# Second-layer weight remainders on VectorE, and one set of statistics for two layer norms, in an attention and mixture-of-experts kernel

## The chip, the cores and the metric

The kernel runs on one core of one Trainium2 chip. A core has TensorE for matmuls, VectorE (DVE), ScalarE (ACT) and GpSimd (POOL) for elementwise work, and SyncE (SP), which here only issues DMAs. Each engine works through its own queue in order, and engines wait for each other through semaphores. The metric is device time in microseconds (us), less is better.

## The reference, cut to what matters

The input has 4 images of 1024 tokens and 256 channels. An image goes through a group norm with attention and a projection, then, as tokens, through a second attention, and then:

```python
t = t + attention(_ln_t(t))
t = t + ffn(_ln_t(t))

def ffn(x):                       # 8 experts, the two best for each token
    x_norm = layernorm(x) * ln_g + ln_b
    combine = weights of the top 2 of softmax(x_norm @ gate_w)
    for e in range(8):
        h = gelu(x_norm @ w1[e] + b1[e])          # 256 -> 1024
        out = out + combine[:, e] * (h @ w2[e] + b2[e])   # 1024 -> 256
    return x + out
```

So two layer norms follow the attention: the first makes x out of t, the second makes x_norm out of x. Both divide by sqrt(variance + 1e-5).

## The kernel before, in words

Every large matmul is made exact enough by splitting both operands into a high half (a rounded fp32r copy) and a low half (value minus high half), and by three passes on TensorE (`three`, line 1567). The high half is usually made by ACT, the low half by DVE.

**Images.** `image` on each engine does one image, b = 0 to 3. The first attention goes over eight row blocks i: TensorE turns the probabilities (L1647), computes the scores of block i+2, and mixes the values of block i-1. On DVE block i is `lo1(i)` (L1277), `max1(i+2)` (L1272), `out1(i-1)` (L1286 to L1295), `norm1(i-2)` (L1300). TensorE's turning of block i+1 waits for `lo1(i)`. On ACT, `hi1(i)` (L812) stands before it.

**The tail of an image**, everything from the attention's sum to x_norm, is spread over the start of the next image; image 3's tail stands alone between attention and routing. It works in halves h of four token tiles. DVE adds the attention result (`tail_add`, L1227) and takes statistics (`tail_stats`, L1238 to L1243: which=0 of t, which=1 of x). POOL makes the scale by a power of -1/2 (L589) and the bias (L614, L615). ACT applies them (`tail_norm`, L776). The sum t + x for the accumulator rows is on POOL (`stream`, L621), and the multiplication by ln_g and the addition of ln_b are on POOL inside the images (`affine`, L626, L628) and on DVE in the last tail (L1462, L1465). SP writes both results to DRAM (`rows_of`: L480 for r_out, and behind it in the same queue L483 for xf). Routing starts when all five engines have signalled their end; SP's comes after both DMAs have landed.

**Routing** builds, from the gate's logits, a table of up to 40 steps, each with one expert and 256 token slots (`route`).

**Expert steps.** Step s uses buffer n = s mod 2. TensorE computes eight chunks f of the first layer, three chunks ahead, and eight of the second. ACT applies the gelu (L971); DVE makes the two halves of its result, the high half by a conversion (`tensor_copy`, L1535) and the low half by a subtraction (L1537). Between chunks, the halves for step s+1 are prepared: if its expert differs from the one in that buffer (`fresh`), both weights are loaded again, 1 MB each, and split in eight pieces of 128x512. ACT makes the high halves of all eight (L931), DVE the low halves of the four first-layer pieces (L1487, at chunks 0, 1, 3, 4) and POOL the low halves of the four second-layer pieces (`split_w2`, L729). POOL's queue also gathers rows for step s+2 (L694) and scatters those of step s-1 (L707), both by indirect DMAs; `split_w2` stands behind them. DVE also adds the second-layer bias (L1508, after chunk 1) and splits the gathered rows (L1499, after chunk 2). Two steps form a turn of a loop; each step reads `fresh` from a table and branches, and each turn reads `live` as well. The pieces of step 0 are made during routing (`first_pieces`, before L1135).

## Time and profile before

| | us |
|---|---|
| median of 3 runs | 1328.66 |
| lowest and highest run | 1323.03, 1333.6 |
| span of the profiled execution | 1323.4 |

No separate total of the profiled execution is given; its span equals the fastest run to within 0.4 us, so what lies around the span is taken as nothing.

| engine | busy us | share of the span |
|---|---|---|
| TensorE matmuls | 1184.0 | 89% |
| VectorE | 874.8 | 66% |
| ScalarE | 545.9 | 41% |
| GpSimd | 414.8 | 31% |

Up to the end of the images TensorE is busy for nine tenths or more of nearly every slice. They take the span up to about 694 us, the last tail runs to 729, routing to 782, the expert steps from there to about 1292, and the output transposes the rest. The chain that ended last is 79% TensorE and 13% VectorE; 71% is line 1567, 7% is the conversion in line 1535. A shared line such as 1567 serves many products, so the tiles beside it say which one is meant. An idle time in brackets counts for the time of the kernel only on the engine that everything else waits for.

### The profile page before, as it was taken

Reading aid. Unit: us, or ns where it says so; the run is one execution under the profiler, and the core shown is the slowest. Engines: PE = TensorE matmul, PEld = TensorE weight load, DVE = VectorE, ACT = ScalarE, POOL = GpSimd, SP = SyncE. Lnnn points to the kernel's source line nnn. Section 1 sums busy time; section 2 is a strip of 40 time slices with the busy share of each in tenths; the row PEclk is TensorE's granted clock in tenths of the full one; section 3 lists DMA queues with packets and bytes.
Section 4 is the critical chain, followed back from the end, with each engine's and each line's share of the span. In section 5 each row is a group of like instructions: output and inputs, shape, how many; then the busy total and the mean of one; then the engine's idle time right before and its main releaser. Section 6 shows DMA issues by size and latency. Waiting matters only on the chain.

```text
span 1323.4 us, 25477 instructions
## 1 busy us (share of the span) xinstructions
PE 1184.0 (89%) x8118; PEld 1099.4 (83%) x8119; DVE 874.8 (66%) x1819; ACT 545.9 (41%) x995; POOL 414.8 (31%) x416
## 2 busy tenths in 40 slices
PE   6999999999999999999993468889879897799992
PEld 5897998989889889898883368789779897799992
DVE  4675477854668537684357968866885868966651
ACT  2432445434344334543333245535544545444431
POOL 0010003400024000240003365665664566644540
PEclk9999999999999999999995688899889899999997
DMA  4000001100001000000001314525433536323337
GB/s 155 1 33 0 1 1 33 64 1 0 2 33 64 0 1 1 33 33 0 1 1 64 135 68 129 154 44 148 146 82 59 168 94 179 96 53 59 56 48 258
DMA packets 66205, 82.69 MB, mean 62 GB/s; under 512 B 11104, under 2 KB 56544, under 8 KB 66144
## 3 DMA queue, kind: packets, MB, share of 16 engines
q1 hardware_dynamic: 52128, 63.48, 14.7%
q0 software_dynamic: 14016, 18.37, 7.7%
q8 instruction: 42, 0.69, 0.2%
q14 instruction: 19, 0.16, 0.0%
HBM read 60.85 MB, written 22.02 MB: 63 GB/s over the span
## 4 chain that ended last, share of the span: by engine, by line
PE 79%; DVE 13%; ACT 2%; issue 2%; DMA 2%; SPq 1%; POOL 1%; ACTq 0%; POOLq 0%; DVEq 0%
PE ps L1567 71%; DVE hs L1535 7%; PE ps L1647 2%; PE ps L1857 1%; PE ps L1609 1%; PE ps L1580 1%; ACT h L971 1%; DVE hs L1537 1%; DVE one_hot L1122 1%; DMA rows<-acc_rows 1%; ACT w2s L931 1%; DVE pick_hi L1130 1%; PE ps L1600 1%; PE ps L1656 1%; PE ps L1669 1%
## 5 line engine op out<-in xcount | busy, mean ns | idle before, releaser
L1567 PE MATMUL ps<-w2s,hs 128*128 128x256 f32 x1728 | 265.6, 291 | 46.9 <-DVE hs L1537 46.5
L1567 PEld LDWEIGHTS ps<-w2s,hs 128*128 128x128 f32 x1728 | 235.9, 198 | 52.3 <-DVE hs L1537 50.0
L1567 PE MATMUL ps<-xt,w1s 128*128 128x256 f32 x1746 | 269.0, 292 | 3.2 <-issue 1.7
L1567 PEld LDWEIGHTS ps<-xt,w1s 128*128 128x128 f32 x1746 | 237.5, 198 | 5.0 <-issue 2.9
L1535 DVE CAST hs<-h 128x256 fp32r<-128x256 f32 x288 | 178.5, 620 | 87.7 <-ACT h L971 45.8
L971 ACT ACTIVATE h<-ps,b1t 128x256 f32<-128x256 f32 x288 | 136.8, 475 | 121.1 <-PE ps L1567 100.9
L707 POOL DMA_INDIRECT acc_rows<-y_w,now_s x72 | 117.6, 1633 | 170.1 <-issue 163.3
L1537 DVE TENSOR_TENSOR hs<-h,hs 128x256 fp32r<-128x256 f32 x288 | 124.2, 431 | 9.9
L589 POOL TENSOR_TENSOR tl_r<-tl_eps,minus_half 128x4 f32<-128x4 f32 x16 | 16.2, 1013 | 350.8 <-DVE tl_eps L1243 350.8
L1567 PE MATMUL ps<-xs,wh 128*128 128x512 f32 x384 | 123.1, 401 | 1.5 <-issue 1.5
L694 POOL DMA_INDIRECT xg<-xf_rows,now_g x76 | 86.8, 1143 | 48.1 <-POOL now_g L690 35.5
L1567 PE MATMUL ps<-vs,pr 128*128 128x256 f32 x768 | 98.1, 283 | 0.0
L1567 PEld LDWEIGHTS ps<-vk,pr 128*128 128x128 f32 x768 | 94.0, 188 | 3.2 <-DVE pr L1384 0.8
L1567 PE MATMUL ps<-xs,qs 128*128 128x512 f32 x384 | 95.5, 397 | 0.0
L1567 PE MATMUL ps<-vk,pr 128*128 128x256 f32 x768 | 94.8, 279 | 0.6 <-DVE pr L1384 0.6
L1567 PE MATMUL ps<-qs,ks 128*128 128x512 f32 x384 | 92.3, 391 | 0.0
L1567 PEld LDWEIGHTS ps<-vs,pr 128*128 128x128 f32 x768 | 92.2, 188 | 0.0
L1379 DVE TENSOR_REDUCE neg_max<-ps 128x1 f32<-128x1024 f32 x32 | 39.2, 1224 | 79.8 <-PE ps L1567 79.8
L729 POOL TENSOR_TENSOR w2s<-w2r,w2s 128x512 fp32r<-128x512 f32 x64 | 88.3, 1774 | 1.1 <-ACT w2s L931 1.1
L1567 PEld LDWEIGHTS ps<-xs,wh 128*128 128x128 f32 x384 | 69.7, 189 | 16.0 <-issue 1.7
L1567 PEld LDWEIGHTS ps<-qs,ks 128*128 128x128 f32 x384 | 70.1, 188 | 13.5
L1567 PEld LDWEIGHTS ps<-xs,qs 128*128 128x128 f32 x384 | 69.7, 188 | 13.6
(213 smaller groups left out, 1908.5 us busy)
## 6 DMA issues: line engine op xcount, KB each, us to landing
w1r<-in_w SPq DMA_DIRECT2D x16, 1024.0 KB, 5.0
w2r<-in_w SPq DMA_DIRECT2D x16, 1024.0 KB, 8.9
b2t<-in_b SPq DMA_DIRECT2D x36, 128.0 KB
xn<-in_x SPq DMA_DIRECT2D x4, 1024.0 KB, 4.9
acc_rows<-r_out SPq DMA_DIRECT2D x4, 1024.0 KB, 4.5
xf_rows<-xf SPq DMA_DIRECT2D x4, 1024.0 KB, 5.0
rows<-acc_rows SPq DMA_DIRECT2D x8, 512.0 KB, 7.4
out_tokens<-cols_out SPq DMA_DIRECT2D x8, 512.0 KB, 9.2
```

Source lines behind the costliest of these rows:

```text
L589: return g.tensor_tensor(dst, src, minus_half[:, 0:src.shape[1]], ALU.pow)
L694: g.indirect_dma_start(out=xg[:, n, h, :], out_offset=None, in_=xf_d, in_offset=bass.IndirectOffsetOnAxis(ap=now_g[:, n, h:h + 1], axis=0) ...
L707: g.indirect_dma_start(out=acc_d, out_offset=bass.IndirectOffsetOnAxis(ap=now_s[:, n, h:h + 1], axis=0), in_=y_w[:, n, h, :], in_offset=No ...
L729: g.tensor_tensor(w2s[n][1][:, :, :].rearrange("p f c -> p (f c)")[:, c], w2r[:, n, c], w2s[n][0][:, :, :].rearrange("p f c -> p (f c)")[: ...
L931: a.copy(dst[:, c], src[:, n, c]).then_inc(ws_act, 1)
L971: a.activation(h32[:, gi % 4, :], bank(gi % 4, STEP), ACT.Gelu, bias=b1t[:, n, f:f + 1]).then_inc(h_act, 1)
L1122: v.tensor_tensor(one_hot[:, j, :], iota[:, 0:COLS].unsqueeze(1).to_broadcast((P, PICK, COLS)), hi_f[:, k, t].unsqueeze(2).to_broadcast((P ...
L1379: v.tensor_reduce(neg_max[:, i:i + 1], bank(2 * (i % 2), count=2), AXX, ALU.max, negate=True).then_inc(s2_max, 1)
L1535: v.tensor_copy(hs[0][:, f, :], h32[:, gi % 4, :]).then_inc(h_hi, 1)
L1537: v.tensor_tensor(hs[1][:, f, :], h32[:, gi % 4, :], hs[0][:, f, :].bitcast(F32), ALU.subtract).then_inc(h_lo, 1)
L1567: ins = t.matmul(out, left[l], right[r], start=first and n == 0, stop=last and n == 2, **more)
L1647: ins = t.transpose(bank(4, count=2)[:, j * P:(j + 1) * P], prob[:, i % 2, j * P:(j + 1) * P], ident[:, :])
```

## The change

Two edits are made at once.

**Edit 1, expert steps.** POOL's `lo_pieces` and `split_w2` are gone. DVE subtracts all eight pieces of a fresh step, in chunks 0, 1, 3, 4, 5, 6 and 7 (two in chunk 7), and the eight of step 0 during routing. `ws_dve` now counts eight pieces.

**Edit 2, the tail.** The sum t goes to a tile of its own, `t1`. One set of statistics (mean m, variance v of t1) serves both norms: POOL raises two numbers per token, v + eps and v(1 + eps) + eps^2, to the power -1/2 in one instruction of twice the size. ACT writes the accumulator rows directly, as t1 times (1 + r) minus m r (`tail_rows`); DVE writes xf in two passes over each tile with ln_g and ln_b in them (`tail_xf`), eight instructions per half. POOL's `stream` and `affine` are gone, and ACT's pass for xf. In the last tail `tail_rows` stands behind ACT's `gate_columns`.

```diff
-        ACT_TAIL = {1: (0, 1), 3: (1, 0), 4: (1, 1)}
-        DVE_TAIL = {2: (1, 0), 3: (1, 1)}
+        DVE_TAIL = {2: 0, 3: 1}
...
+            def tail_scales(b, h):
+                c = slice(4 * h, 4 * h + 4)
+                pool.wait_ge(tl_in, at(b, 2, h + 1))
+                g.tensor_tensor(tl_r[:, :, c], tl_eps[:, :, c],
+                                minus_half[:, :].rearrange("p (k t) -> p k t", k=2), ALU.pow).then_inc(tl_own, 1)
+                pool.wait_ge(tl_own, at(b, 2, h + 1))
+                g.tensor_tensor(tl_nb[:, c], tl_nm[:, c], tl_r[:, 0, c], ALU.mult).then_inc(tl_out, 1)
+                g.tensor_tensor(tl_s[:, c], tl_r[:, 0, c], ones[:, 0:4], ALU.add).then_inc(tl_out, 1)
...
-                    lo_pieces(s + 1, 1 - n, (i if n == 0 else i + 1))
...
+            def tail_rows(b, h):
+                act.wait_ge(tl_out, at(b, 4, 2 * h + 2))
+                if not (isinstance(b, int) and b == 0):
+                    act.wait_ge(tok_out, at(b, 16, 0))
                 for j in range(4 * h, 4 * h + 4):
-                    ins = a.activation(dst[:, j, :], src[:, j, :], ACT.Identity,
-                                       bias=tl_nb[:, which, j:j + 1], scale=tl_r[:, which, j:j + 1])
-                ins.then_inc(ready, 1)
+                    ins = a.activation(r_out[:, j, :], t1[:, j, :], ACT.Identity,
+                                       bias=tl_nb[:, j:j + 1], scale=tl_s[:, j:j + 1])
+                ins.then_inc(r_ready, 1)
...
-            for which in range(2):
-                for h in range(2):
-                    tail_norm(B - 1, which, h)
             for h in range(2):
                 gate_columns(B - 1, h)
+            for h in range(2):
+                tail_rows(B - 1, h)
...
+                v.tensor_scalar(tl_eps[:, 1, cs], tl_mv[:, cs, 1], 1.0 + LN_EPS, LN_EPS * LN_EPS,
+                                ALU.mult, ALU.add)
+                v.tensor_scalar(tl_nm[:, cs], tl_mv[:, cs, 0], -1.0, None, ALU.mult)
+                v.tensor_scalar(tl_eps[:, 0, cs], tl_mv[:, cs, 1], LN_EPS, None, ALU.add).then_inc(tl_in, 1)
+
+            def tail_xf(b, h):
+                dve.wait_ge(tl_own, at(b, 2, h + 1))
...
+                for j in range(4 * h, 4 * h + 4):
+                    step(v.scalar_tensor_tensor(xf[:, j, :], t1[:, j, :], tl_mv[:, j, 0:1], g_row[:, :],
+                                                ALU.subtract, ALU.mult))
+                settle()
+                for j in range(4 * h, 4 * h + 4):
+                    ins = v.scalar_tensor_tensor(xf[:, j, :], xf[:, j, :], tl_r[:, 1, j:j + 1], b_row[:, :],
+                                                 ALU.mult, ALU.add)
+                ins.then_inc(xf_ready, 1)
...
                 def out1(i):
                     w(av_mm, NT, i + 1)
-                    if i == 0 and not first:
-                        w(r_ready, 2, 0)
...
-            W_AT = (0, 1, 3, 4)
+            W_AT = {0: (0,), 1: (1,), 3: (2,), 4: (3,), 5: (4,), 6: (5,), 7: (6, 7)}
...
             def first_pieces():
-                for f in range(4):
+                for f in range(8):
                     w_piece(0, 0, 0, f)
...
-                    if split and f in W_AT:
-                        w_piece(s + 1, 1 - n, (i if n == 0 else i + 1), W_AT.index(f))
+                    if split:
+                        for piece in W_AT.get(f, ()):
+                            w_piece(s + 1, 1 - n, (i if n == 0 else i + 1), piece)
```

What the edits do to the order of instructions, at three places. First, GpSimd in the expert loop behind the scatter, with a fresh step to come. Before (the last two rows come twice more):

```order
L707 DMA acc_rows<-y_w,now_s 4096x256 x2
L716 ISA
L716 TENSOR_LOAD fresh
L716 ISA x2
L716 COMPARE_AND_BRANCH
L723 ISA
L725 ISA
L727 REGISTER_ALU
L729 TENSOR_TENSOR w2s<-w2r,w2s 128x512
L727 REGISTER_ALU
L729 TENSOR_TENSOR w2s<-w2r,w2s 128x512
L727 REGISTER_ALU
```

and now, where the next gather follows the scatter directly:

```order
L661 DMA acc_rows<-y_w,now_s 4096x256 x2
L644 ISA
L644 COPY now_g<-gather_at 128x2
L645 REGISTER_ALU
L648 DMA xg<-xf_rows,now_g 128x256 x2
```

The table read, the branch and the four subtractions behind the scatter are gone.

Second, VectorE in chunks 6 and 7 of such a step (REGISTER_ALU rows prepare the number that the next instruction waits for). Before:

```order
L1535 CAST hs<-h 128x256
L1537 TENSOR_TENSOR hs<-h,hs 128x256
L1532 REGISTER_ALU
L1535 CAST hs<-h 128x256
L1537 TENSOR_TENSOR hs<-h,hs 128x256
```

and now:

```order
L1473 CAST hs<-h 128x256
L1475 TENSOR_TENSOR hs<-h,hs 128x256
L1423 REGISTER_ALU
L1427 TENSOR_TENSOR w2s<-w2r,w2s 128x512
L1470 REGISTER_ALU
L1473 CAST hs<-h 128x256
L1475 TENSOR_TENSOR hs<-h,hs 128x256
L1423 REGISTER_ALU
L1427 TENSOR_TENSOR w2s<-w2r,w2s 128x512
L1423 REGISTER_ALU
L1427 TENSOR_TENSOR w2s<-w2r,w2s 128x512
```

One second-layer piece now follows chunk 6 and two follow chunk 7; one more follows chunk 5.

Third, VectorE in row block i = 2 of an image that carries a tail, from `norm1(0)` to `lo1(3)`. Before:

```order
L1300 TENSOR_SCALAR tn<-tok,ln_mv,ln_r 128x256
L1238 BN_STATS tl_bn<-x 128x6 x4
L1156 REGISTER_ALU
L1161 MEMSET spare 128x1
L1241 BN_AGGR tl_mv<-tl_bn 128x2 x4
L1156 REGISTER_ALU
L1243 TENSOR_SCALAR tl_eps<-tl_mv 128x4
L1277 TENSOR_TENSOR pr<-ps,pr 128x1024
```

and now (`t` is the tile t1):

```order
L1243 TENSOR_SCALAR tn<-tok,ln_mv,ln_r 128x256
L1181 REGISTER_ALU
L1183 SCALAR_TENSOR_TENSOR xf<-t,tl_mv,g_row 128x256 x4
L1086 REGISTER_ALU
L1187 SCALAR_TENSOR_TENSOR xf<-xf,tl_r,b_row 128x256 x4
L1222 TENSOR_TENSOR pr<-ps,pr 128x1024
```

Where statistics of x stood ahead of `lo1(3)`, the eight instructions of `tail_xf(0)` stand now.

## Rows read from the trace of the kernel before

**Rows 1.** Windows with fresh weights, one and the sum of four: us, busy us per engine, PEclk.

```profile
914.90:985.20 70.30, 57.21 (x420) 55.52 (x419) 60.41 (x89) 36.28 (x78) 44.87 (x41) 0.89 0.49 142
...
sum 246.00, PE 199.69 PEld 193.58 DVE 211.75 ACT 126.11 POOL 156.59; mean PE 49.92 PEld 48.40 DVE 52.94 ACT 31.53 POOL 39.15
```

**Rows 2.** The same view: a pair of steps with reused weights, and step 0.

```profile
1218.00:1241.50 23.50, 23.50 (x202) 23.50 (x201) 14.34 (x36) 9.91 (x22) 12.02 (x12) 1.00 0.33 56
786.50:799.80 13.30, 10.99 (x87) 10.20 (x86) 12.36 (x21) 8.33 (x19) 9.88 (x10) 1.00 0.51 179
```

**Rows 3.** The same windows, conversions of line 1535 alone.

```profile
sum 246.00, DVE 118.79; mean DVE 29.70
```

**Rows 4.** The reused pair, conversions of line 1535 alone.

```profile
1218.00:1241.50 23.50, 5.33 (x16) 1.00 0.33 56
```

**Rows 5.** Instructions of line 729 (count: shortest/median/longest ns).

```profile
L729 POOL TENSOR_TENSOR w2s<-w2r,w2s x64: 1270/1827/1873, 781.3 to 1155.5; 128x512 fp32r<-128x512 f32 x64
```

**Rows 6.** Timeline of a step with fresh weights: start, duration, engine [idle before it].

```profile
924.80 6.35 DVE L1535 CAST hs<-h 128x256 fp32r<-128x256 f32 x1
...
925.47 5.52 POOL L729 TENSOR_TENSOR w2s<-w2r,w2s 128x512 fp32r<-128x512 f32 x4
...
931.67 1.03 PE L1567 MATMUL ps<-w2s,hs 128*128 128x256 f32 x6 [3.46 <-DVE hs L1537]
...
933.57 0.35 DVE L1535 CAST hs<-h 128x256 fp32r<-128x256 f32 x1 [1.96 <-PE ps L1567]
```

**Rows 7.** Timeline of VectorE a little later, back to back.

```profile
936.17 0.68 DVE L1487 TENSOR_TENSOR w1s<-w1r,w1s 128x512 fp32r<-128x512 f32 x1
936.77 0.28 DVE L1535 CAST hs<-h 128x256 fp32r<-128x256 f32 x1
```

**Rows 8.** Timeline, first row block of an attention image that carries a tail.

```profile
374.95 2.08 ACT L776 ACTIVATE x<-tok,tl_nb,tl_r 128x256 f32<-128x256 f32 x4 [1.38 <-POOL tl_nb L615]
...
377.96 1.23 DVE L1277 TENSOR_TENSOR pr<-ps,pr 128x1024 fp32r<-128x1024 f32 x1 [0.98 <-ACT pr L812]
...
379.34 1.06 PE L1647 MATMUL ps<-ident,prob 128*128 128x128 f32 x8
```

**Rows 9.** Timeline, the row blocks i = 2 and 3 of the same image.

```profile
395.02 1.40 DVE L1238 BATCH_NORM_STATS2 tl_bn<-x 128x6 f32<-128x256 f32 x4
...
396.95 1.22 DVE L1277 TENSOR_TENSOR pr<-ps,pr 128x1024 fp32r<-128x1024 f32 x1
...
399.41 1.03 PE L1647 MATMUL ps<-ident,prob 128*128 128x128 f32 x8
...
401.66 1.40 DVE L1238 BATCH_NORM_STATS2 tl_bn<-x 128x6 f32<-128x256 f32 x4
```

**Rows 10.** Instructions that write tl_r.

```profile
L589 POOL TENSOR_TENSOR tl_r<-tl_eps,minus_half x16: 1006/1014/1018, 204.1 to 707.2; 128x4 f32<-128x4 f32 x16
```

**Rows 11.** Instructions of line 1396.

```profile
L1396 DVE SCALAR_TENSOR_TENSOR vk<-v,row_inv,vk x32: 483/484/487, 145.4 to 688.7; 128x256 fp32r<-128x256 f32 x32
```

**Rows 12.** Timeline of the last tail.

```profile
700.64 0.17 DVE L1243 TENSOR_SCALAR tl_eps<-tl_mv 128x4 f32<-128x4 f32 x1
...
708.73 5.63 POOL L621 TENSOR_TENSOR r_out<-tok,x 128x1024 f32<-128x1024 f32 x2
...
708.82 3.34 DVE L1462 TENSOR_TENSOR xf<-xf,g_row 128x1024 f32<-128x1024 f32 x1
...
716.60 1.23 DVE L1465 TENSOR_TENSOR xf<-xf,b_row 128x1024 f32<-128x1024 f32 x1
...
719.89 1.01 ACT L782 COPY xfT<-ps 128x1024 f32<-128x1024 f32 x1 [1.33 <-PE ps L1600]
...
728.94 0.23 POOL L669 IOTA iota_i<- 128x128 int32 x1 [14.59 <-DVEq L1472]
```

**Rows 13.** DMA issues of the page: count, KB each, median microseconds to landing.

```profile
xf_rows<-xf SPq DMA_DIRECT2D x4, 1024.0 KB, 5.0
```

**Rows 14.** Timeline, end of the routing tables.

```profile
772.88 0.24 DVE L1135 COPY slot_w<-ps 128x80 f32<-128x80 f32 x1 [0.20 <-PE ps L1843]
```

More of the change, by code:

```diff
@@ L650, in image @@
             def image(b, first, last):
                 if not first:
-                    last_norms(b - 1, lambda i: first_norm(b, i))
-                for i in range(0 if first else 4, NT):
+                    for h in range(2):
+                        tail_scales(b - 1, h)
+                for i in range(NT):
                     first_norm(b, i)
@@ L662, in _ @@
             image(B - 1, False, True)
-            last_norms(B - 1, lambda i: None, affines=False)
+            for h in range(2):
+                tail_scales(B - 1, h)
             pool.wait_ge(tl_out, 4 * B)
@@ L830, in image @@
                 else:
-                    tail_norm(b - 1, 0, 0)
+                    tail_rows(b - 1, 0)
                     hi1(0)
@@ L839, in image @@
                         hi1(i)
-                    if not first and i in ACT_TAIL:
-                        tail_norm(b - 1, *ACT_TAIL[i])
+                    if not first and i == 1:
+                        tail_rows(b - 1, 1)
                     if i + 2 < NT:
@@ L898, in _ @@
             act.wait_ge(xf_out, (B - 1) * 16)
-            for which in range(2):
-                for h in range(2):
-                    tail_norm(B - 1, which, h)
             for h in range(2):
                 gate_columns(B - 1, h)
+            for h in range(2):
+                tail_rows(B - 1, h)
             act.wait_ge(xf_col, 2 * B)
@@ L1349, in image @@
                 if not first:
-                    w(xf_ready, 2, 0)
                     w(tok_out, 16, 0)
@@ L1451, in _ @@
             tail_add(B - 1, 0)
-            tail_stats(B - 1, 0, 0)
+            tail_stats(B - 1, 0)
             tail_add(B - 1, 1)
-            tail_stats(B - 1, 0, 1)
-            tail_stats(B - 1, 1, 0)
+            tail_stats(B - 1, 1)
+            tail_xf(B - 1, 0)
+            tail_xf(B - 1, 1)
             tops(range(0, NT))
-            tail_stats(B - 1, 1, 1)
             tops(range(NT, 2 * NT))
-            for h in range(2):
-                c = slice(4 * h, 4 * h + 4)
-                dve.wait_ge(xf_norm, 2 * (B - 1) + h + 1)
-                step(v.tensor_tensor(xf[:, c, :], xf[:, c, :],
-                                     g_row[:, :].unsqueeze(1).to_broadcast((P, 4, C)), ALU.mult))
-                settle()
-                v.tensor_tensor(xf[:, c, :], xf[:, c, :],
-                                b_row[:, :].unsqueeze(1).to_broadcast((P, 4, C)), ALU.add).then_inc(xf_ready, 1)
             tops(range(2 * NT, 3 * NT))
```

139 lines of the change are left out of this document (34 added, 105 removed).

## The prediction

> **What bounds the kernel now.** I read the slices first (TensorE is at nine tenths or more through the images, then falls to 5 to 8 in places from 786 us on), then sums over windows in the expert steps, then the timeline of one step, and at last the tail and the start of an image, where edit 2 acts.
>
> The expert steps come in two kinds. Line 729 ran 64 times [rows 5], four times per fresh set, so 16 sets: one before step 0, one in step 0, and 14 in the four windows whose sum is 246.0 us [rows 1]. A step that prepares fresh weights takes 246.0 / 14 = 17.6 us. A step without them takes 23.5 / 2 = 11.75 us, and there TensorE is busy for all of the 23.50 [rows 2]: that is TensorE's own pace. A fresh step loses 5.8 us.
>
> The timeline shows where [rows 6]. GpSimd's four subtractions run from 925.47 for 5.52 us; VectorE's conversion, begun at 924.80, lasts 6.35 us instead of some 0.3 and ends when they end. TensorE waits 3.46 us for the low half behind it, and afterwards its clock is at the lower of its two levels (1.2 instead of 2.4 GHz) for a while: the granted share is 0.89 over 914.9 to 985.2 and 1.00 in the reused pair [rows 1, 2]. Over the four windows these conversions cost 118.79 us [rows 3]; at the 5.33 us per 16 of the reused pair [rows 4] the 112 would cost 37.3. So edit 1 takes away 81 us of VectorE time on a path that TensorE waits for, and gives VectorE 2.4 us of work per step back.
>
> **Edit 1, the fresh step.** VectorE may now be the bound, so I add up what it has to do in one step:
> - all but conversions: (211.75 - 118.79) / 14 = 6.64 us [rows 1, 3];
> - eight conversions undisturbed: 5.33 / 2 = 2.67 us [rows 4];
> - four more pieces: VectorE starts its next instruction 0.60 us after a piece although the piece lasts 0.68 [rows 7], so 4 x 0.60 = 2.4 us;
> - the start of a step: table reads and branches leave VectorE idle, 1.96 us at the start of a turn [rows 6] (the row names TensorE, which had long been done with what is waited for; the time is the sequencer's). The second step of a turn has one of the two reads, an estimate of half, 1.0; the mean is 1.5 us.
>
> Together 13.2 us, more than TensorE's 11.75. VectorE becomes the bound of fresh steps. I take 13.4, with 0.2 for waits that do not line up. 14 x (17.6 - 13.4) = 58.8 us. Step 0 takes 13.30 [rows 2]; without a step start its VectorE work is 11.7, so about 12.3: 1.0 us. **Edit 1 gives -60 us in the steps.** Bounds: at best VectorE's work overlaps fully and TensorE's 11.75 holds (-82); at worst one more wait like a step start, 2 us, sits in each step (-31). VectorE now also waits, at chunk 5, for the second-layer weights to arrive, with chunk 6 queued behind; ScalarE waits for the same weights at chunk 4 already, so that this is not a new end. Reloading does not move: the loads for a buffer wait for all its pieces, but these end a full step ahead. GpSimd's gathers come earlier, and nobody waits for them.
>
> The Trainium skill (VectorE: DVE Perf Modes, The DRAIN you can't avoid) says that the next instruction does not start until the pipeline has emptied. By that a piece would cost its full 0.68 us, 0.3 us more per step, and the gain would be some 4 us smaller. The rows show starts 0.60 apart, so I do not take it.
>
> During routing four more pieces stand ahead of the copy that reads the finished table. It starts 0.20 us after TensorE's last product [rows 14], with nothing to spare: **+2.4 us** (2.4 to 2.8).
>
> **Edit 2, inside the images.** Images are bound by TensorE, so what leaves GpSimd and ScalarE there is worth nothing. What is added can cost, since two chains have little slack.
> - Start of the image: ScalarE's `tail_norm` starts at 374.95 and takes 2.08, `hi1(0)` and `lo1(0)` follow, the latter ends at 379.18, and TensorE turns block 1 at 379.34 [rows 8]. The power on GpSimd grows from four numbers per partition, 1.01 us [rows 10], to eight: between 1.01 and 2.03, and I take 1.6 since one instruction has a fixed part. With two more tiny VectorE instructions ahead (0.1 to 0.2), this chain comes 0.7 us later, and TensorE with it.
> - Block 2: the statistics take 1.93 us, 395.02 to 396.95, and `lo1(3)` then ends at 398.17 for a turn at 399.41 [rows 9]. `tail_xf` is eight instructions of 0.484 [rows 11], 0.40 apart: 3.3 us. `lo1(3)` ends at 399.6: +0.3.
> - Block 3: from `lo1(3)` at 396.95 to the tail's start at 401.66 is 4.7 us with 0.26 of waiting [rows 9], so VectorE now needs 4.45 + 3.3 = 7.75 us in a block that TensorE finishes in 6.7 (399.41 to the next turn, 406.1). Another +1.1.
>
> 2.1 us in each of three images, **+6.3 us** (0 to 12, if the slack is there after all, or if each is met by a GpSimd power). The wait of `out1(0)` for `r_out` goes; late next there is TensorE's value product. `tail_rows` waits for the DMA of an image earlier, `tail_xf` for powers taken a block earlier: both long done.
>
> **Edit 2, the last tail**, all of it exposed. Statistics of the second half end at 700.81 [rows 12], with four tiny instructions more at 701.2. `tail_xf` twice is 6.7 us: xf ready at 707.9, instead of 716.60 + 1.23 = 717.8 [rows 12]. From there to routing it takes 11.1 us (728.94), which would be a gain of 9.9. But the accumulator rows now come last: ScalarE copies the gate's columns until 3.1 us after xf is ready (720.90 against 717.83 [rows 12]), so `tail_rows` runs 711.0 to 715.2. SP issues that DMA first and xf's about 0.6 behind it. One such DMA lands in 5.0 us alone [rows 13]; two at once in 5 to 10, I take 9. SP's end comes at 724.8, **-4 us** (-2 to -10).
>
> A GpSimd instruction can hold VectorE up here: VectorE's multiplication at 708.82 lasted 3.34 us while GpSimd's sum, begun at 708.73, ran [rows 12]; one of the same shape undisturbed takes about 1.2 (the last addition, 1.23). `tail_xf(0)` starts just as GpSimd begins the second power, and could lose up to its 1.6 us, which lies in the -2. The Trainium skill (SBUF — State Buffer, Who interferes with whom) has the same as a rule: the pair of ports that the two engines share goes to whoever starts first for the whole instruction, and VectorE instructions with two SBUF inputs contend with GpSimd ones that read. By that the last tail would give -2.5.
>
> **Sum.** -60 + 2.4 + 6.3 - 4 = -55 us against the execution's 1323.4: 1268. The median lies 5.3 us above it: **1273 us**.
>
> **Rivals.**
> - TensorE-bound after all: VectorE's instructions pack better and fresh steps reach about 12.2. 14 x 1.2 us less: 1256. For it: nothing in a step depends on chunk 7's pieces at once. Against it: the sum of 13.2. 12%.
> - GpSimd still disturbs: it issues four indirect DMAs per step, and a VectorE that never idles meets them more often. If each costs VectorE 0.7 us, steps take 16.2: 1312. The Trainium skill's rule above makes this possible for conversions. Against it, the undisturbed mean is 0.33 us where the shortest conversion is 0.28 [rows 4, 7], with these DMAs running. 8%.
> - The edit does less than it says, since the wait moves to ScalarE (its pieces and gelus) or to the arrival of weights: steps of 14.8, 1293. ScalarE's busy time is 126.11 / 14 = 9.0 us per step [rows 1], well under. 7%.
> - **Slower.** TensorE's clock. Behind its long waits it runs at half speed for a while; now it would have a short wait in nearly every chunk. At half clock throughout, TensorE needs up to 2 x 11.75 = 23.5 us for a step, so fresh steps would be slower than their 17.6 from half of the work at half clock; at all of it 14 x 5.9 = +83 in place of -59, some 1415. Against it: step 0, with 10.99 of 13.30 us busy and waits spread, kept 1.00 [rows 2]. 4%.
>
> My forecast has the other 69%; its own range is 1262 to 1288. To leave out no more than two in ten, with the bounds of edit 1, the range is **1252 to 1302**. What a measurement of this kernel can tell from no change is about 1%, 13 us: faster 0.94, within it 0.02, slower 0.04.
>
> **What would show it.** Right: no conversion over about 0.8 us; fresh steps near 13.4 with VectorE idle only at step starts; full clock through the expert steps; `lo1(4)` late for TensorE's turn by about 1 us; routing started by SP. Wrong: fresh steps near 12 (packing), or half clock with short waits (the slower rival), or conversions of 1 us beside indirect DMAs.

## The result, and the profile after

| | before | after | predicted |
|---|---|---|---|
| median of runs, us | 1325.97 (4 runs) | 1260.45 (1258.30 to 1261.02, 4 runs) | 1273 (1252 to 1302) |
| ratio to before | | 0.951 [0.948, 0.953] | 0.960 |
| profiled execution, span, us | 1323.4 | 1258.9 | |
| TensorE clock granted, mean | 0.946 | 0.967 | |

Faster by 4.9%, inside the range and 12.6 us under the forecast. I divided both spans at the same five places: the last product of the images, the first instruction of routing, the first low half of step 0, the first low half of step 1, and the last low half.

| stretch, us | before | after | difference | predicted |
|---|---|---|---|---|
| to the last product of the images | 694.10 | 703.42 | +9.3 | +6.3 |
| last tail | 34.84 | 28.36 | -6.5 | -4 |
| routing, first gather, first products | 57.57 | 62.86 | +5.3 | +2.4 |
| step 0 | 13.29 | 11.56 | -1.7 | -1.0 |
| steps 1 to 35 | 486.30 | 415.42 | -70.9 | -58.8 |
| output | 37.27 | 37.29 | 0 | 0 |

**The steps.** The first view sums the engines over all steps (columns as in [rows 1]); it is the answer to [rows 1], of before first and then of after:

```profile
786.51:1286.10 499.59, 450.97 (x3571) 444.07 (x3570) 372.55 (x706) 234.24 (x512) 288.13 (x273) 0.94 0.41 103
```

```profile
794.63:1221.61 426.98, 423.37 (x3575) 421.41 (x3575) 317.07 (x766) 233.66 (x513) 220.41 (x211) 1.00 0.48 115
```

TensorE is busy for 423.37 of 426.98 us, at full clock throughout (0.94 before). The steps are 72.6 us shorter, and both things that the prediction named have a share: TensorE's busy time for the same products fell by 27.6 us (450.97 to 423.37), which is its clock, and its waits for low halves of the hidden layer fell by 41.4 (45.0 to 3.6, below). VectorE makes 60 instructions more (706 to 766) and is busy for 55 us less. Where those went is in the conversions, which answer [rows 3] and [rows 5]. The groups of VectorE over the steps (count, busy us, mean ns, idle time ahead):

```profile
L1475 DVE TENSOR_TENSOR hs<-h,hs 128x256 fp32r<-128x256 f32 x288 | 123.1, 427 | 9.9
L1473 DVE CAST hs<-h 128x256 fp32r<-128x256 f32 x287 | 89.9, 313 | 68.3 <-ACT h L901 31.5 <-PE ps L1506 28.7 <-DVEq L1462 7.7
L1427 DVE TENSOR_TENSOR w1s<-w1r,w1s 128x512 fp32r<-128x512 f32 x60 | 41.1, 685 | 3.7 <-ACT w1s L861 3.7
L1427 DVE TENSOR_TENSOR w2s<-w2r,w2s 128x512 fp32r<-128x512 f32 x60 | 39.8, 684 | 0.0
```

The mean conversion lasts 313 ns; the longest of all 288 lasts 589 ns, where it was 6364. TensorE's wait for low halves of the hidden layer (the 3.46 us of [rows 6]) was 45.0 us in 14 waits over steps 1 to 34, and is:

```profile
PE ps L1506 <- DVE hs L1475: 3.6, 8, 0.7
```

(us in all, times, longest.) Windows over the same 14 fresh steps as in [rows 1], now VectorE alone (length, busy):

```profile
806.18:856.90 50.72, 45.84 (x104) 1.00 0.59 168
...
sum 178.82, DVE 160.28; mean DVE 40.07
```

VectorE's work is 160.28 / 14 = 11.45 us per fresh step. A window ends where VectorE ends, a little behind TensorE, and the steps that follow catch up; so the step's length is better taken from the whole: steps 1 to 34 last 404.9 us (806.2 to 1211.1), 20 of them reused at 11.75 [rows 2]; the 14 fresh ones have (404.9 - 235.0) / 14 = **12.14 us**. In the same way those of before had (475.9 - 235.0) / 14 = 17.2.

The starts of two steps, one in the middle of a turn of the loop and one at its start (they answer the 1.96 us of [rows 6]):

```profile
926.09 1.28 DVE L1427 TENSOR_TENSOR w2s<-w2r,w2s 128x512 fp32r<-128x512 f32 x2
927.29 0.29 DVE L1473 CAST hs<-h 128x256 fp32r<-128x256 f32 x1
...
938.37 1.28 DVE L1427 TENSOR_TENSOR w2s<-w2r,w2s 128x512 fp32r<-128x512 f32 x2
940.61 0.29 DVE L1473 CAST hs<-h 128x256 fp32r<-128x256 f32 x1 [0.95 <-PE ps L1506]
```

In the middle of this turn of the loop VectorE does not pause at all; at the start of the next it pauses for 0.95 us. I had 1.0 and 2.0.

**The images.** The waits of TensorE over images 2 to 4 have one new kind, six times, two in each image:

```profile
PE ps L1586 <- DVE pr L1222: 4.3, 6, 0.7
```

The two chains behind it in one image, where [rows 8] and [rows 9] were:

```profile
376.68 1.65 POOL L596 TENSOR_TENSOR tl_r<-tl_eps,minus_half 128x8 f32<-128x8 f32 x1 [73.68 <-DVE tl_eps L1175]
...
378.87 2.08 ACT L707 ACTIVATE r_out<-t,tl_nb,tl_s 128x256 f32<-128x256 f32 x4 [2.11 <-POOL tl_s L600]
...
381.88 1.23 DVE L1222 TENSOR_TENSOR pr<-ps,pr 128x1024 fp32r<-128x1024 f32 x1 [1.71 <-ACT pr L743]
...
383.25 0.52 PE L1586 MATMUL ps<-ident,prob 128*128 128x128 f32 x3 [0.73 <-DVE pr L1222]
```

```profile
406.65 1.67 DVE L1183 SCALAR_TENSOR_TENSOR xf<-t,tl_mv,g_row 128x256 f32<-128x256 f32 x4
408.36 1.67 DVE L1187 SCALAR_TENSOR_TENSOR xf<-xf,tl_r,b_row 128x256 f32<-128x256 f32 x4
409.95 1.22 DVE L1222 TENSOR_TENSOR pr<-ps,pr 128x1024 fp32r<-128x1024 f32 x1
...
411.32 1.06 PE L1586 MATMUL ps<-ident,prob 128*128 128x128 f32 x8 [0.74 <-DVE pr L1222]
```

The first: power, rows, high half, low half, turn, each handing its delay on. The second: `tail_xf` ahead of `lo1(4)`. But six waits are 4.3 us, and the images take 9.3 more. A part of the rest has no wait in front of it: TensorE's products themselves are slower. Over the first image, which carries no tail at all, before (L1567) and after (L1506), with count, busy us and mean ns:

```profile
L1567 PE MATMUL ps<-vs,pr 128*128 128x256 f32 x192 | 24.5, 283 | 0.0
L1567 PE MATMUL ps<-vk,pr 128*128 128x256 f32 x192 | 23.7, 279 | 0.0
...
L1506 PE MATMUL ps<-vs,pr 128*128 128x256 f32 x192 | 24.9, 286 | 0.0
L1506 PE MATMUL ps<-vk,pr 128*128 128x256 f32 x192 | 24.3, 283 | 0.0
```

The mean distance from start to start at full clock, over all images, goes for `vk`·`pr` from 118.0 to 120.8 ns, for `vs`·`pr` from 121.1 to 123.3, for `wh`·`us` from 116.4 to 121.8.

**The last tail.** It answers [rows 12]:

```profile
712.53 0.43 POOL L600 TENSOR_TENSOR tl_s<-tl_r,ones 128x4 f32<-128x4 f32 x1
...
715.88 1.01 ACT L713 COPY xfT<-ps 128x1024 f32<-128x1024 f32 x1 [17.89 <-PE ps L1539]
...
719.96 4.04 ACT L707 ACTIVATE r_out<-t,tl_nb,tl_s 128x256 f32<-128x256 f32 x8
...
724.08 0.37 SPq L476 DMA_DIRECT2D acc_rows<-r_out  x1
...
724.56 0.52 SPq L479 DMA_DIRECT2D xf_rows<-xf  x1
...
731.77 0.23 POOL L623 IOTA iota_i<- 128x128 int32 x1 [18.81 <-SPq L489]
```

As forecast, SP starts the routing, 7.2 us after it issued the second DMA. ScalarE could have written half of the rows from 709.2 and the rest from 713.0 on, yet waits, idle for 17.89 us, for the gate's columns first.

**Routing.** It answers [rows 14]:

```profile
775.47 2.48 DVE L1427 TENSOR_TENSOR w2s<-w2r,w2s 128x512 fp32r<-128x512 f32 x4
777.88 0.23 DVE L1065 COPY slot_w<-ps 128x80 f32<-128x80 f32 x1
...
779.59 0.38 SPq L505 DMA_DIRECT2D w1r<-in_w  x1
780.07 0.41 SPq L507 DMA_DIRECT2D w2r<-in_w  x1
780.22 1.32 POOL L648 DMA_INDIRECT xg<-xf_rows,now_g  x1 [1.09 <-issue]
...
788.22 1.09 PE L1796 MATMUL ps<-ident,xg 128*128 128x128 f32 x4 [12.52 <-DMA xg<-xf_rows,now_g]
```

The four pieces take their 2.4 us ahead of the copy. Then something that the prediction did not see: TensorE waits for the first gather, and now two weight loads of 1 MB each are issued just ahead of it. From the gather's issue to the turn it takes 8.0 us. In the kernel before it took 4.6, 775.23 to 779.79:

```profile
775.23 1.32 POOL L694 DMA_INDIRECT xg<-xf_rows,now_g  x1 [1.09 <-issue]
...
787.93 0.38 SPq L511 DMA_DIRECT2D w1r<-in_w  x1
```

There SP was still waiting for GpSimd's pieces of step 0, and issued the loads 12.7 us behind the gather.

### The profile page after: what moved, and what is told of

Read it like the earlier page. It is cut to its first block, busy times and chain, and to the rows that moved or that the text cites. A ratio compares the mean times of both kernels' runs of the same rounds, so it can differ in the third digit from the quotient of the medians.

```text
span 1258.9 us, 24947 instructions
## 1 busy us (share of the span) xinstructions
PE 1161.5 (92%) x8118; PEld 1081.5 (86%) x8119; DVE 817.7 (65%) x1879; ACT 529.3 (42%) x963; POOL 289.9 (23%) x307
## 4 chain that ended last, share of the span: by engine, by line
PE 77%; DVE 11%; DMA 3%; issue 3%; ACT 2%; SPq 1%; POOL 1%; DVEq 1%; ACTq 0%; POOLq 0%
PE ps L1506 71%; PE ps L1586 2%; PE ps L1796 1%; DVE xf L1183 1%; DVE xf L1187 1%; PE ps L1519 1%; DVE pr L1222 1%; DMA w1r<-in_w 1%; ACT r_out L707 1%; PE ps L1548 1%; DVE w2s L1427 1%; DMA rows<-acc_rows 1%; DVE hs L1473 1%; DVE one_hot L1052 1%; DVE pick_hi L1060 1%
## 5 line engine op out<-in xcount | busy, mean ns | idle before, releaser
L1506 PE MATMUL ps<-xt,w1s 128*128 128x256 f32 x1746 | 258.4, 284 | 1.5 <-DVE xt L1437 1.5
L1506 PE MATMUL ps<-w2s,hs 128*128 128x256 f32 x1728 | 251.6, 281 | 3.6 <-DVE hs L1475 3.6
L1506 PEld LDWEIGHTS ps<-xt,w1s 128*128 128x128 f32 x1746 | 228.2, 190 | 2.2 <-DVE xt L1437 1.9
L1506 PEld LDWEIGHTS ps<-w2s,hs 128*128 128x128 f32 x1728 | 224.0, 188 | 5.2 <-issue 5.2
L661 POOL DMA_INDIRECT acc_rows<-y_w,now_s x72 | 121.2, 1683 | 166.0 <-issue 154.9
L1473 DVE CAST hs<-h 128x256 fp32r<-128x256 f32 x288 | 90.2, 313 | 71.8 <-ACT h L901 35.1
L1506 PE MATMUL ps<-xs,wh 128*128 128x512 f32 x384 | 123.1, 401 | 1.6 <-issue 1.6
L648 POOL DMA_INDIRECT xg<-xf_rows,now_g x76 | 92.6, 1218 | 47.3 <-POOL now_g L644 34.7
L1506 PE MATMUL ps<-vs,pr 128*128 128x256 f32 x768 | 99.7, 286 | 0.0
L1506 PEld LDWEIGHTS ps<-vk,pr 128*128 128x128 f32 x768 | 96.2, 191 | 3.2 <-DVE pr L1326 0.8
L1506 PE MATMUL ps<-vk,pr 128*128 128x256 f32 x768 | 97.1, 283 | 0.6 <-DVE pr L1326 0.6
L1506 PE MATMUL ps<-xs,qs 128*128 128x512 f32 x384 | 95.4, 397 | 0.0
L1506 PEld LDWEIGHTS ps<-vs,pr 128*128 128x128 f32 x768 | 94.0, 191 | 0.0
L1506 PE MATMUL ps<-qs,ks 128*128 128x512 f32 x384 | 92.4, 391 | 0.0
L596 POOL TENSOR_TENSOR tl_r<-tl_eps,minus_half 128x8 f32<-128x8 f32 x8 | 13.3, 1664 | 342.1 <-DVE tl_eps L1175 342.1
L1506 PEld LDWEIGHTS ps<-xs,wh 128*128 128x128 f32 x384 | 69.8, 189 | 16.2 <-issue 1.8
L1506 PEld LDWEIGHTS ps<-qs,ks 128*128 128x128 f32 x384 | 70.3, 188 | 13.5
L1506 PEld LDWEIGHTS ps<-xs,qs 128*128 128x128 f32 x384 | 69.8, 188 | 13.5
L1506 PE MATMUL ps<-xs,wl 128*128 128x512 f32 x192 | 76.1, 397 | 0.0
```

Of the source, the lines that this page charges most:

```text
L596: g.tensor_tensor(tl_r[:, :, c], tl_eps[:, :, c], minus_half[:, :].rearrange("p (k t) -> p k t", k=2), ALU.pow).then_inc(tl_own, 1)
L648: g.indirect_dma_start(out=xg[:, n, h, :], out_offset=None, in_=xf_d, in_offset=bass.IndirectOffsetOnAxis(ap=now_g[:, n, h:h + 1], axis=0) ...
L661: g.indirect_dma_start(out=acc_d, out_offset=bass.IndirectOffsetOnAxis(ap=now_s[:, n, h:h + 1], axis=0), in_=y_w[:, n, h, :], in_offset=No ...
L1473: v.tensor_copy(hs[0][:, f, :], h32[:, gi % 4, :]).then_inc(h_hi, 1)
L1506: ins = t.matmul(out, left[l], right[r], start=first and n == 0, stop=last and n == 2, **more)
```

## The experiments

Each was measured beside the kernel before, whose median was 1325.0 to 1325.2 each time; the changed kernel itself has only the four runs above. Times are medians; lengths of stretches are from the profiled execution of each.

### Either edit alone

Edit 1 alone is the kernel before with `w_piece` of eight pieces and no `lo_pieces`; edit 2 alone is the rest of the diff.

> The kernel before with edit 1 alone: VectorE makes all eight low halves, the tail of the images stays as it was. Theory (the two edits do not touch each other): the steps gain 72.7 us as in the changed kernel, the routing loses 5.3 us (four more pieces ahead of the table copy, and SP's two weight loads for step 2 issued ahead of the first gather), images and last tail stay: 67.4 us less, about 1258.6 us; TensorE's value products in the images keep their pitch of 118.0 and 121.1 ns. Rival 1: part of the step gain comes from edit 2 (addresses, an earlier start of the weights), then under 65 us. Rival 2: the 5.3 us of the routing come from edit 2, then about 72 us less, 1254 us.

> The kernel before with edit 2 alone: one set of statistics, GpSimd keeps its four pieces in the steps. Theory: images +9.3 us (six stalls of TensorE of 0.65 to 0.74 us, and value products 2 to 3 ns slower each), last tail -6.4 us, steps and routing as before: +2.9 us, about 1328.9 us. Rival: the slower products in the images belong to edit 1 or to the whole program's layout; then images +4.5, sum -2 us, 1324 us.

Edit 1 alone: **1252.75 us**, ratio 0.947 [0.945, 0.948]; images 693.3, last tail 31.7, routing to the first low half 63.0, step 0 and the others 425.4. Edit 2 alone: **1330.69 us**, ratio 1.004 [1.003, 1.006]; images 704.2, last tail 28.4, routing 57.6, steps 501.1. Together -72.4 + 5.5 = -66.9, where both at once gave -65.5: they add up to within 1.4 us, and each term lies in the edit that I had put it under, the late gather in edit 1 (8.15 us from its issue to the turn), the slower products in edit 2. **Edit 2 costs 5.5 us by itself; the kernel is better without it.**

Edit 1 alone gained 72.4 us where I expected 67.4. 1.5 us of the difference lie in the steps, and 3.1 in the last tail, in which nothing is changed. The window of the gate's 32 products (busy us, granted clock), before and with edit 1 alone:

```profile
719.65:726.49 6.84, 6.83 (x33) 0.50 0.35 115
```

```profile
718.88:722.60 3.72, 3.72 (x33) 0.96 0.64 212
```

TensorE has come out of a wait of over 20 us shortly before. In the one execution its clock is up for these products, in the other it stays at the lower level until behind them. Four traces have this tail in unchanged code: it lasts 34.8 us in the kernel before and in the one shifted by 32 bytes (below), and 31.7 with edit 1 alone and in the first try on the conversions (below). I take that for luck; with one trace of each kernel it is not shown that it is not a trait of the kernel. After the change SP's DMAs end last, and it does not matter.

### Addresses put back

```diff
+        pad_a = sb("pad_a", [P, 8])
         logits = sb("logits", [P, TILES, E])
...
+        pad_b = bs("pad_b", [P, 72])
         xf = bs("xf", [P, NT, C])
```

Edit 2 drops `minus_one` (32 bytes per partition) and shrinks the `tl_` tiles by 288, and all tiles that are allocated later move down: weights and probabilities by 32 bytes, `vs`, `vk`, `us` by 320.

> The changed kernel with two unused tiles (8 and 72 floats per partition) that put every tile of the images back to the address it had in the kernel before; no instruction changes. Theory A (TensorE's products in the images are slower because their operands moved by 32 bytes): products of vk with pr return from 120.8 to 118.0 ns start to start, vs with pr from 123.3 to 121.1, wh with us from 121.8 to 116.4, and the images end some 5 us earlier: 1255.5 us. Theory B (they are slower because of what the other engines now do beside them): no change, 1260.5 us, pitches stay.

**1256.45 us**, 4.0 less than the changed kernel, and the pitches are back at 118.1, 120.8 and 116.5 ns. The same view of the first image as above:

```profile
L1508 PE MATMUL ps<-vs,pr 128*128 128x256 f32 x192 | 24.5, 283 | 0.0
L1508 PE MATMUL ps<-vk,pr 128*128 128x256 f32 x192 | 23.7, 279 | 0.0
```

The distance between the first turns of two images (and from the last one to the images' end) is the cleanest measure, since it leaves out the start of the program, which varies by 1.9 us (41.98 to 43.89 us to the first turn, over all kernels here):

| us | image 1 | image 2 | image 3 | image 4 | sum |
|---|---|---|---|---|---|
| before | 162.54 | 169.25 | 167.42 | 151.13 | 650.3 |
| after | 163.80 | 172.49 | 170.53 | 154.15 | 661.0 |
| addresses put back | 162.53 | 171.70 | 169.32 | 152.99 | 656.5 |
| before, shifted by 32 bytes | 162.63 | 169.47 | 167.49 | 151.17 | 650.8 |

Theory A holds: of +10.6 us in the images **4.4 are addresses alone** and 6.2 are edit 2's work. (The same code differs by up to 1.0 us in such a sum from one trace to another: 650.3 to 651.3 where the images are those of before.)

> The kernel before with its 32-byte constant for minus one placed behind the small tiles of the images, so that weights, probabilities and values of the images stand 32 bytes lower, as in the changed kernel, and those behind the small tiles stay; no instruction changes. Theory A (addresses): the pitches of vk with pr and of vs with pr rise by 2 to 3 ns and the images end 3 to 5 us later: 1330 us. Theory B (work of the other engines): no change, 1326 us.

**1327.51 us**, ratio 1.001 [0.999, 1.003]: no difference that can be told. `vk`·`pr` rises by 1.0 ns, `vs`·`pr` falls by 1.2; only `wh`·`us` rises by 2.7, half of its 5.4, and it is a small group. So for the value products it is not the 32 bytes by themselves; the 320 by which `vs`, `vk` and `us` moved, or how they and `pr` now stand to each other, does it. That is left open.

### The tail's place inside the images

`tail_xf` now takes two tiles at a time, so that it has four parts:

```diff
-        DVE_TAIL = {2: 0, 3: 1}
+        DVE_TAIL = {2: 0, 3: 1, 4: 2, 5: 3}
...
-                    tail_rows(b - 1, 0)
                     hi1(0)
...
-                    if not first and i == 1:
-                        tail_rows(b - 1, 1)
+                    if not first and i in (1, 3):
+                        tail_rows(b - 1, i // 2)
```

> The realigned kernel (tiles of the images back at their old addresses) in which, inside the images, ScalarE makes the accumulator rows in blocks 1 and 3 instead of ahead of the first high half, and VectorE makes the layer norm in four parts of two tiles in blocks 2 to 5 instead of two parts of four tiles in blocks 2 and 3. Theory: both stalls of TensorE in each image (0.73 us at the turn of block 1 and 0.74 at that of block 5) go: 4.3 us less than the realigned kernel, images end at 696, 1252.2 us. Rival: the stall at block 5 is not the length of that part but a wait of the whole chain through VectorE, which only moves: half of it, 1254.3 us.

**1253.14 us**, 3.3 less than the realigned kernel. The waits:

```profile
PE ps L1588 <- DVE pr L1224: 1.2, 3, 0.4
```

4.5 us in six waits have become 1.2 in three, one at the turn of block 7 in each image. The images' four distances sum to 652.4, 4.2 less than with addresses put back (6.2 of extra work down to 2.0). The theory gets the two stalls right and misses a small third one.

### The accumulator rows first

```diff
             for h in range(2):
+                tail_rows(B - 1, h)
+            for h in range(2):
                 gate_columns(B - 1, h)
-            for h in range(2):
-                tail_rows(B - 1, h)
```

> The changed kernel in which ScalarE, in the last tail, writes the accumulator rows (half 0 can start at 709.2, half 1 at 713.0) ahead of the gate's columns, for which it waits idle until 715.88. Theory: the rows are ready at 715.1 instead of 724.0, SP's end of the tail comes some 4 us earlier and the routing is started by VectorE (its tops end at 727.7) or by the DMA of xf: 2 to 4 us less, last tail 24.5 to 26.5 us instead of 28.4, 1257 us. Rival: both DMAs are bound by xf, issued at 724.56 only because it stands behind the other on SP; if xf is ready no earlier, the tail keeps its 28.4 us: 1260.5 us.

**1255.9 us**, 4.5 less; the last tail takes 24.67 us instead of 28.36, which is 3.7 of it. Its DMAs are issued at 714.82 and 716.74, and the routing is started by VectorE:

```profile
727.75 0.23 POOL L623 IOTA iota_i<- 128x128 int32 x1 [15.13 <-DVEq L1406]
```

### The gather first

```diff
+                    sp.wait_ge(g_in[n], at(u, SUB * 16, 0))
+                    sp.sem_inc(sp_held, 1)
                 e = sp.value_load(expert_of[0:1, bass.ds(s, 1)], ...)
...
-                for f in range(8):
+                for f in range(4):
                     w_piece(0, 0, 0, f)
             route(dve, v, first_pieces)
+            for f in range(4, 8):
+                w_piece(0, 0, 0, f)
```

> The changed kernel with two edits of the passage from routing to step 0: VectorE makes the four second-layer pieces of step 0 behind the tables instead of ahead of the copy that reads them, and SP issues the weights of steps 2 and 3 only once the gathers of steps 0 and 1 have landed. Theory: TensorE waits for the first gather (12.52 us); the pieces ahead of the table delay it by 2.4 us, and the two weight loads issued at 779.59 and 780.07, ahead of the gather at 780.22, by the rest (it lands 6.3 us after its issue, 2.8 us before the change); images end to first turn of gathered rows gets 5.3 us shorter, the gather lands about 3 us after its issue again: 1255.2 us. Rival: the gather's 6.3 us have nothing to do with the loads (the engine's own start, or the row order); then only the 2.4 us: 1258 us.

**1257.23 us**, 3.2 less by the medians; the stretch itself, from the start of routing to the first turn of gathered rows, takes 51.26 us instead of 56.45 (50.85 before), 5.2 less. The profile:

```profile
779.95 1.32 POOL L650 DMA_INDIRECT xg<-xf_rows,now_g  x1 [1.09 <-issue]
...
784.54 1.08 PE L1800 MATMUL ps<-ident,xg 128*128 128x128 f32 x4 [7.37 <-DMA xg<-xf_rows,now_g]
...
786.01 0.38 SPq L507 DMA_DIRECT2D w1r<-in_w  x1
```

Its two parts can be told apart. From the start of routing to the first gather's issue: 46.3 us before, 48.5 after, 46.7 here; that is the pieces. From its issue to the turn: 4.6, 8.0 and 4.6 again; that is the loads, which are now issued 6.1 us behind it. Counted from the start of routing, the weights of step 2 come 4.9 us later than in the changed kernel, and nobody misses them.

### Two more pieces on VectorE

```diff
+                if f in (2, 5) and not (isinstance(s, int) and s == 0):
+                    v.tensor_tensor(extra[:, f // 4, :], raw_w[:, n, c], hi[:, c].bitcast(F32), ALU.subtract)
```

> The changed kernel with two more pieces on VectorE in each fresh step (pieces 2 and 5 are made a second time, into a tile that nobody reads), 1.2 us by their pitch. Theory A (VectorE is the bound of a fresh step, as the prediction had it): 15 x 1.2 = 18 us more, 1278 us. Theory B (TensorE is the bound and VectorE has slack of a microsecond or more): no more than 3 us more, 1262 us. In between the rise over 15 steps, taken from 1.2, is VectorE's slack per fresh step.

**1275.97 us**, +15.5. TensorE's waits for low halves rise from 3.6 us to

```profile
PE ps L1509 <- DVE hs L1478: 9.5, 15, 0.8
```

and steps 1 to 34 take 418.6 us: (418.6 - 235.0) / 14 = 13.11 us for a fresh step, 0.97 more for 1.2 us of work. VectorE's slack was 0.2 us. Theory A, nearly to the end: in a fresh step VectorE and TensorE need the same time within a few tenths.

### What held the conversions

The first try was to part GpSimd's four pieces in the kernel before:

```diff
                 for f in range(4, 8):
                     pool.wait_ge(ws_act, at(s, 8, f + 1))
+                    if not (isinstance(s, int) and s == 0):
+                        pool.wait_ge(h_lo, at(s, FC, 2 * (f - 4) + 1 - FC))
```

> The kernel before, in which GpSimd's four second-layer pieces of a step no longer run back to back: each also waits for one more low half of the hidden layer (chunks 0, 2, 4, 6 of the running step). The same work on the same engines. Theory A (a conversion on VectorE is held for as long as GpSimd instructions follow each other without a pause, 6.35 us in one piece): now each hold ends with its piece, no conversion lasts over some 1.7 us, VectorE loses at most 4 x 1.1 us per fresh step and TensorE rides over the short holds: fresh steps 15 us, total 1290 us. Theory B (the four pieces cost VectorE 5.5 us however they lie): conversions still sum to some 118 us over the fresh steps, TensorE waits as long in all: 1320 to 1330 us.

**1321.37 us**, ratio 0.997 [0.995, 0.999]. It tests neither theory: GpSimd gets to its pieces only in chunk 7 of the step, when all four waits are met, and runs them back to back as before. In the profiled executions 3.1 of the 5.5 us of difference are the last tail's; where the 3.6 us between the medians come from is not shown. A conversion is held as before:

```profile
838.34 6.35 DVE L1537 CAST hs<-h 128x256 fp32r<-128x256 f32 x1
...
839.00 5.53 POOL L731 TENSOR_TENSOR w2s<-w2r,w2s 128x512 fp32r<-128x512 f32 x4
```

The second was to add work of this kind to the changed kernel, on tiles of its own, at the start of each step; the spaced kernel has no `if` there, and waits for chunk k, `n * FC + k + 1`:

```diff
                     s = i * 2 + n
+                    for k in range(4):
+                        if k == 0:
+                            pool.wait_ge(h_lo, at(i, 2 * FC, n * FC + 1))
+                        g.tensor_tensor(g_dst[:, k, :], g_src[:, :], g_src[:, :], ALU.subtract)
                     gather(s + 2, n, False)
```

> The changed kernel with four subtractions of 128x512 added on GpSimd in every step, back to back behind chunk 0, on tiles that nobody else uses and whose result nobody reads. Theory A (GpSimd's elementwise work holds VectorE through the ports they share, also where the data have nothing to do with each other): one instruction of VectorE per step lasts 5 to 6 us; fresh steps 12.1 + 5 = 17 us, reused steps 12 to 15 us, some 1350 us in all (1320 to 1400). Theory B (VectorE's long conversions in the kernel before were the tiles' affair: a bank or a wait on the same weights): nothing changes, 1262 us.

**1333.13 us**, 73 more than the changed kernel, within theory A's bounds. One of 15 holds of over 4 us:

```profile
921.12 1.57 POOL L664 DMA_INDIRECT acc_rows<-y_w,now_s  x1 [0.31 <-issue]
...
921.95 4.96 DVE L1482 CAST hs<-h 128x256 fp32r<-128x256 f32 x1
922.17 4.58 POOL L679 TENSOR_TENSOR g_dst<-g_src 128x512 fp32r<-128x512 f32 x4
```

and the other kind, in most fresh steps, where the two engines alternate:

```profile
939.17 0.69 DVE L1436 TENSOR_TENSOR w1s<-w1r,w1s 128x512 fp32r<-128x512 f32 x1
939.18 5.26 POOL L679 TENSOR_TENSOR g_dst<-g_src 128x512 fp32r<-128x512 f32 x4 [3.56 <-DVE hs L1484]
...
939.78 1.13 DVE L1482 CAST hs<-h 128x256 fp32r<-128x256 f32 x1
...
940.95 1.14 DVE L1484 TENSOR_TENSOR hs<-h,hs 128x256 fp32r<-128x256 f32 x1
```

GpSimd's work holds VectorE where they share no data: a conversion of 0.29 us lasts 1.13 or 4.96.

Which of the two happens goes with what GpSimd does just ahead. 16 of the 36 groups of four start while the indirect DMA in front of them still shows as running, some 0.5 us before its end, as at 922.17 above. Each of them holds an instruction of VectorE to the end of the group: 15 for over 4 us, and one, begun late in the group, for 2.17. The other 20 groups start 0.15 us or more behind that DMA (at 939.18 after 3.56 us of waiting), and beside them no instruction of VectorE lasts over 1.53 us. The kernel before shows the same: its 14 holds of 5.6 to 6.4 us all belong to pieces that start inside the scatter, and the one group that starts after a wait, at 790.96 in step 0, alternates with VectorE (1.38, 1.39 and 1.77 us). This is an order read from traces. Why it is so is not shown, and no kernel that keeps the pieces on GpSimd but away from the scatter was run.

> As the kernel with four subtractions in a row, but GpSimd now waits for one more low half of the hidden layer ahead of each (chunks 0 to 3), so that they can't follow each other without VectorE getting through a chunk. Theory A (a hold lasts as long as GpSimd instructions queue up without a pause): no instruction of VectorE lasts over 1.7 us; reused steps are back at 11.75 us, fresh steps at 12.1 + 4 x 0.8 = 15.3 or less: 1310 us. Theory B (the holds sum to the same 5 us however they lie): fresh steps as with four in a row.

**1349.35 us**, 16 more than four in a row. Both of its theories fall. Instructions of VectorE still last 3 us and more (the longest conversion 4.0), since in a reused step GpSimd comes late, finds its waits met, and three pieces follow each other and the scatter anyway. Here too the 34 groups that start inside an indirect DMA hold an instruction of VectorE for 1.8 to 4.0 us, and the 64 single ones that start after a wait for no more than 1.2. That GpSimd's queue falls further behind with the waits in it would explain the rest, but is argued, not shown. Spacing is no cure here.

### All repairs together

The realigned kernel with the spread tail, the rows first and the gather first.

> All repairs together: tiles of the images at their old addresses, the spread tail inside the images, the accumulator rows first in the last tail, the second-layer pieces of step 0 behind the tables and the weights of steps 2 and 3 behind the first gathers. If they add up: 1253.1 (the realigned kernel with the spread tail) - 5.2 (as measured for the late load) - 3 (rows first) = 1245 us. Rival: the last tail gives nothing, 1248 us.

**1244.99 us** (1244.08 to 1245.36), ratio 0.939 [0.938, 0.941]: the expected 1245. Images 695.8, last tail 24.9, routing 57.6, steps 426.3. It is 15.5 us better than the change as it was, and 7.8 better than edit 1 alone. Edit 1 with the repair of the gather, and without edit 2, was not run; an estimate from 1252.75 and the 5.2 us of that repair is 1247.5, so what edit 2 is worth with all its repairs, some 2.5 us by this estimate, is not shown.

## Why the prediction was right, and where it was not

**The mechanism of edit 1 held**: the conversions go back to 0.3 us, the clock to full, the wait of 3.46 us goes. That GpSimd's work was what held them was an inference from overlapping rows; the added subtractions on foreign tiles show it. The Trainium skill (SBUF — State Buffer, Who interferes with whom) gives the reason, one pair of ports shared by the two engines, and says that whoever starts first has it for its whole instruction. The turns of 1.13 us agree; a hold through four instructions, 4.96 and 6.35 us, is more than the rule says. Of the gain in the steps the clock was the smaller share (27.6 us) and the waits the larger (41.4).

**The step that failed is the size of a fresh step**, 13.4 against 12.14. By its terms:
- the start of a step, taken at 1.5 us, is 0.6 on average, **0.9 us too much** in each. Ahead of its first conversion VectorE pauses for 0.94 to 1.08 us at the start of a turn of the loop; in the middle of a turn it pauses for 0 to 0.18 us behind a fresh step and for some 0.6 in the three cases behind a reused one. My 1.96 and 1.0 are what the changed kernel still shows from one reused step to the next (2.07 and 0.93), where VectorE has nothing queued. Behind a fresh step two pieces, 1.28 us of work, stand in its queue, and its sequencer runs ahead: in the middle of a turn the branch is taken while the last piece still runs. The Trainium skill (Perfetto Trace Analysis, Per-engine timelines) has this: VectorE's instructions wait in a queue behind the sequencer, which goes on to the next; the traces agree;
- the work itself, taken at 6.64 + 2.67 + 2.4 = 11.7, is 11.45. The section of the Trainium skill that I held against the 0.60 per piece (VectorE: DVE Perf Modes, The DRAIN you can't avoid) goes on that a next instruction that is not held starts earlier; the trace agrees, with starts 0.60 us apart (926.09 and 926.69) where a piece lasts 0.68;
- the 0.2 for waits that do not line up has 0.06 against it, which is what remains: 11.45 + 0.63 + 0.06 = 12.14.

14 x 1.26 = 17.6 us too little gain; the fresh step before was 17.2 and not 17.6 once the catching up of the steps behind it is counted, which takes 5.6 back, and step 0 gave 0.7 more: -72.6 where I had -60.

**The number owes something to luck.** The steps gave 12.8 us more than forecast and the last tail 2.5; the images cost 3.0 more and the routing 2.9, and these misses partly cancel to 9.4. The other 3 or 4 us are the 5.3 by which I put the median above the profiled execution: after the change it is 1.5 (1260.45 against 1258.9), and with one run more the kernel before has 2.6. The measured 1260.45 lies nearer to the first rival's 1256 than to my 1273.

The rival "TensorE-bound after all" had 12.2 us for a step and 12%. Its 12.2 was right and TensorE is busy for 99% of the steps; but two more pieces cost nearly their full time, so VectorE is the bound just as much. I should have given the neighbourhood of 12 more: the estimates for the two engines, 13.2 and 11.75, were 1.45 apart, and the larger one was 1.1 too high.

**Routing**: +2.4 for the pieces was about right (2.2 by the gather's issue). Missing is 3.4 for the gather (0.3 came back in other places), which the code of the kernel before shows plainly: SP waited for GpSimd's pieces ahead of a load, GpSimd was late with them, and that wait kept 2 MB off the queues while the gather ran. I wrote "reloading does not move", having looked at whether the weights come in time and not at what their DMAs run beside.

**Inside the images**: +6.3 was predicted and 6.2 measured, addresses apart. From turn to turn in image 3: turn 0 to 1 went from 3.78 to 4.50 us (+0.72, predicted 0.7), turn 3 to 4 from 6.70 to 6.91 (+0.21; 0.3), turn 4 to 5 from 6.70 to 7.66 (+0.96; 1.1), 5.7 us in three images. The power of eight numbers took 1.66 us (1.6). Not seen at all were the 4.4 us of addresses.

**Last tail**: -6.5 where -4 was predicted, SP's end at 731.8 with images that ended 9.3 later, that is at 722.4 on the clock of before, against my 724.8. The term that was mis-sized is the two DMAs at once: SP's end came 7.7 us after it issued the first of them and not 9.6. And `tail_xf(0)` was not held at all (1.67 us for four, at 0.40 each). The range of -2 to -10 had it.

**The slower rivals** did not show: full clock through the steps although TensorE waits eight times for up to 0.7 us; no conversion over 0.59 beside indirect DMAs.

## What to carry to other kernels

- Elementwise work moved off VectorE to GpSimd is not free time: 0.3 us conversions lasted 1.1 to 6.4 beside it. The long holds came where the elementwise work started inside an indirect DMA of the same queue. Moved back, each piece of 1.38 us on GpSimd cost VectorE 0.60, until VectorE's sum came up against TensorE's.
- For each wait that an edit removes, ask what it kept apart. Here an accidental one held 2 MB of loads behind a gather that TensorE waited for: 3.4 us.
- An edit that saves work off the bound can still cost it: three fewer passes over a tile made the images 10.6 us longer, 6.2 by what now stands ahead of a turn and 4.4 by where the tiles lie. After any change in the list of tiles compare the mean of an untouched product.

## What the runs showed of the hardware

- The same product of 128x256 takes 118.0 or 120.8 ns start to start, depending on where its tiles lie in SBUF; 80 unused floats per partition brought back 4.0 us of 1260. A shift of 32 bytes of one operand alone did not do it (+1.0 and, for the other value product, -1.2 ns). The products of the steps (118.3 and 119.8 ns) did not change with it.
- Elementwise instructions that GpSimd starts while its indirect DMA ahead still shows as running hold an instruction of VectorE until the last of them ends (4.96 us for four on foreign tiles, 6.35 in the kernel before; 16 of 16 groups in the one trace, 14 of 14 beside a busy VectorE in the other). Started 0.15 us or more behind it, they alternate with VectorE at some 1.13 us each (20 of 20 groups). The reason is left open.
- 32 products shortly behind a wait of over 20 us took 3.72 us at a granted clock of 0.96 or 6.83 at 0.50, in stretches of identical work, two traces with each: 3.1 us of a run can be this.
